# Latent attention with rotary scores: the low rotary products of two score tiles in the two halves of the array's rows, and one set of rotary tables

## The chip, the cores and the metric

The kernel runs on one core of a Trainium2 chip. A core has a matrix engine (PE; its weight loads are listed apart as PEld), a vector engine (DVE), an activation engine (ACT), GpSimd (POOL) and a queue of its own for issuing transfers (SP). Each engine runs its instructions in order and waits on counting semaphores. The metric is the device time of one execution in microseconds; less is better.

## The reference

One transformer block on x of 2048 rows and 512 columns. The layer norm of x is xn. The result is x + attention(xn) + linear(xn), where the linear part uses a weight rounded to three values and adds a bias. The attention has 16 heads, a shared latent key of 128 columns and a shared rotary key of 64 columns:

```python
q = (x @ wq.T).reshape(B, S, N_HEADS, QK_HEAD)
q_nope, q_pe = (q[..., :NOPE], q[..., NOPE:])
q_pe = apply_rope(q_pe, cos, sin)
kv = x @ wkv_a.T
kv_lat, k_pe = (kv[..., :KV_RANK], kv[..., KV_RANK:])
k_pe = apply_rope(k_pe[:, :, None, :], cos, sin)[:, :, 0, :]
q_lat = jnp.einsum('bshd,hdc->bshc', q_nope, wkv_b_h[:, :NOPE])
kv_cache = rmsnorm(kv_lat, kv_norm_w)
scores = (jnp.einsum('bshc,btc->bsht', q_lat, kv_cache) + jnp.einsum('bshr,btr->bsht', q_pe, k_pe)) * SCALE
attn = jax.nn.softmax(jnp.where(causal, scores, NEG_INF), axis=-1)
out_lat = jnp.einsum('bsht,btc->bshc', attn, kv_cache)
out = jnp.einsum('bshc,hdc->bshd', out_lat, wkv_b_h[:, NOPE:])
return out.reshape(B, S, N_HEADS * VDIM) @ wo.T
```

## The kernel before

The program has two parts. The first (`build_prepare`, up to about 195 us) makes the layer norm, the keys and the folded weights of all heads, and stores them in memory. The second (`build_attention`) is the attention, and the change is nearly all in it.

**Precision by parts.** A float32 number is held as a high part and a low part in the fast 32-bit format (fp32r), and a product a*b is made as high*high + high*low + low*high. So the latent part of a score tile takes three products of 128 rows of the array: (q_h, Kn_h), (q_h, Kn_l), (q_l, Kn_h). The rotary part has 64 rows only. `Kp` holds the high rotary key in partitions 0 to 63 and the low one in 64 to 127; `qp_h` holds the high rotary query twice, `qp_l` the low one twice. So (qp_h, Kp) gives high*high + high*low in one product of 128 rows, and (qp_l, Kp) gives low*high, and low*low with it.

**Tiles and order.** The 2048 queries are cut into NCH = 4 chunks of 512, a chunk into QB = 4 blocks of 128. In chunk j, a head has 4(j+1) score tiles ("units" u): query block i = u // (j+1) against key block b = u % (j+1), of 512 keys, or of 128(i+1) keys on the diagonal (b = j), which also gets a product with the mask (L1000). Over 16 heads and 4 chunks that makes 640 tiles. Two PSUM buffers, `p_score[u % 2]`, take the tiles in turn.

`walk` goes from head to head; one call of `step(cur, prev, nxt)` on each engine does the scores of head cur, the transposes and value products of head prev, and the projections of head nxt. On PE a step is, for every unit u: `scores(cur, u)` (L996, L1000), `transposes(prev, u)` of the probabilities (L1013, four of 128 columns, fewer in the last four tiles), `values(prev, u-2)` (L1025, three products); the rotary projection of nxt (L976, 12 products) stands once in every second step, at the unit that `rotary_unit` gives (half way; unit 1 in chunk 0). Behind the units come the latent projection of nxt (four groups of three products, L976, "q" below) with the last two value groups between them, and then the output projection (12 products, L1036).

**DVE** does for every unit, in this order: `copy_scores` (L1081), which waits for `scored`, copies the tile into `probs` and takes its maximum; on the diagonal `neg_max` (L1087); then `split_tile` (L1093), the low part of the transposed tile of prev, for which ACT makes the high part (L1173). The five rotary operations of nxt (L1104, L1108) follow behind the unit of the rotary projection, three in one unit and two in the next. **PE waits** for DVE in two ways here: `scores(u)` waits until tile u-2 is copied, `values(k)` until tile k is split, and `transposes(k)` until tile k-3 is split.

**SP** loads the weights of each head a head ahead; the tables `cosT` and `sinT` of a chunk have two buffers each, and are loaded with the residual `acc` long before the chunk.

Of the kernel before, what the change touches and what calls it, by code (L numbers as in the profile page):

```python
# [120 lines left out]
def build_prepare(nc, t, keep, stored):  # L121
# [4 lines left out]
    with ExitStack() as ctx:  # L126
        def sb(name, shape, dt=F32):
            return ctx.enter_context(nc.sbuf_tensor(name, shape, dt))
# [7 lines left out]
        ident, xT, residual = keep["ident"], keep["xT"], keep["acc0"]  # L136
        Wq, Wp, Wv = keep["Wq"], keep["Wp"], keep["Wv"]
        w_ffn = sb("w_ffn", [P, IT, D])
        ffnT_h = sb("ffnT_h", [P, IT, D], F32R)
# [270 lines left out]
        def _(act):  # L410
# [59 lines left out]
            act.dma_start(rows[:, D:], t["kv_norm_w"].rearrange("(a n) -> a n", a=1)).then_inc(s_const, 16)  # L470
            act.dma_start(keep["order_f32"][:, :], t["order"]).then_inc(s_const, 16)
            act.dma_start(keep["mask_f32"][:, :], t["mask"]).then_inc(s_const, 16)
            act.dma_start(w_ffn[:, :, :], t["w_ffn"].rearrange("(a p) i -> p a i", p=P)).then_inc(s_w, 16)
            act.wait_ge(s_const, 16 * 6)
            act.activation(keep["mask"][:, :], keep["mask_f32"][:, :], ACT.Copy)
            act.activation(keep["ident16"][:, :], ident[:, :], ACT.Copy)
            act.activation(order[:, :], keep["order_f32"][:, :], ACT.Copy).then_inc(s_order, 1)

# [325 lines left out]
def build_attention(nc, t, keep, stored):  # L804
    with ExitStack() as ctx:
# [10 lines left out]

        cosT = [keep["cosT"], sb("cosT1", [P, CW])]
        sinT = [keep["sinT"], sb("sinT1", [P, CW])]
        acc = [keep["acc0"], sb("acc1", [P, QB, D])]
# [26 lines left out]
        p_result = p_tr + [p_out]  # L846

        xT_in = sem("xT_in")
        tables_in = sem("tables_in")
        wq_in = [sem(f"wq_in{i}") for i in range(2)]  # L850
        wp_in = sem("wp_in")
# [28 lines left out]
        def _(sp):  # L880
# [33 lines left out]


            for i in range(2):
# [7 lines left out]
            for j in range(NCH):  # L924
                if j:
                    load_rotary((j, 0, 0))
                    load_q((j, 0, 0))
                    load_v((j - 1, H // 2 - 1, 0))
                    load_chunk(j)
                    load_q((j, 0, 1))  # L930
                    load_v((j - 1, H // 2 - 1, 1))
                load_rotary((j, 1, 0))
                for p in range(2):
                    load_q((j, 1, p))
                    if j:
                        load_v((j, 0, p))
                if j:
                    store_chunk(j - 1)
                if j + 1 < NCH:
                    load_tables(j + 1)  # L940
# [11 lines left out]
        def _(pe):  # L952
# [26 lines left out]

            def scores(pos, u):  # L980
                j, p = pos[0], pos[2]
                i, b = u // (j + 1), u % (j + 1)
                width = P * (i + 1) if b == j else CW
                if u == 0:
# [4 lines left out]
                rows, keys = slice(i * P, (i + 1) * P), slice(b * CW, b * CW + width)  # L989
                out = p_score[u % 2]  # L990
# [48 lines left out]
            def step(cur, prev, nxt):  # L1039
# [29 lines left out]
            for it in range(IT):  # L1069
                project_latent((0, 0, 0), it)  # L1070
            walk(nc, ENG.PE, step)

        @block.vector
        def _(dve):
# [21 lines left out]
            def rotate(pos, op):  # L1096

                if op == 0:
                    if first_of_chunk(pos):
                        need(dve, tables_in, 48 * pos[0])  # L1100
# [3 lines left out]
                    dve.tensor_tensor(rot_cos[:, :], p_rot[:, :], cosT[pos[0] % 2][:, :], ALU.mult)  # L1104
                else:
                    q = op - 1
                    to, of = slice(HALF * q, HALF * (q + 1)), slice(HALF * (q ^ 1), HALF * ((q ^ 1) + 1))
                    last = dve.tensor_tensor(rot_sin[to, :], p_rot[of, :], sinT[pos[0] % 2][of, :], ALU.mult)  # L1108
                    if op == 4:
                        last.then_inc(rot_read, 1)  # L1110
# [10 lines left out]
            def accumulate(pos):  # L1121
                g, p = heads_before(pos), pos[2]
                a = acc[pos[0] % 2]
                dve.wait_ge(exped, rows_before(pos) + QB)
                need(dve, accumulated, QB * g)
# [138 lines left out]
def build(nc, t):  # L1264
    with ExitStack() as ctx:
        def sb(name, shape, dt=F32):
# [5 lines left out]
            "mask": sb("mask_bf16", [P, P], BF16),  # L1272
            "mask_f32": sb("mask_f32", [P, P]),
            "order_f32": sb("order_f32", [P, ROPE]),
            "Kn_h": sb("Kn_h", [P, S], F32R),
# [68 lines left out]
```

## Time and profile before

| | us |
|---|---|
| median of three runs | 1972.43 (1972.4 to 1973.72) |
| span of the profiled execution | 1972.3 |
| PE busy in it | 1911.1 (97%) |
| PE weight loads | 1596.1 (81%) |
| DVE busy | 1277.8 (65%) |
| ACT busy | 887.7 (45%) |
| POOL busy | 317.0 (16%) |
| chain that ended last, PE's share | 81% |

The span of the profiled execution and the median of the runs are the same within 0.2 us, so a change of the span is read as a change of the time. A product of 512 columns is listed with about 0.39 us, but the next one starts 0.23 us behind it: they overlap in the engine. What one costs is the distance from start to start, not its listed duration.

### The profile page before, as it was taken

The page shows a single profiled execution, that of the slowest core. Times are in us where ns is not written, and L with a number is a line of the kernel's source. Part 1 is how long each engine was busy: PE and PEld are TensorE (multiplying, and loading weights), DVE is VectorE, ACT ScalarE, POOL GpSimd, SP SyncE. Part 2 cuts the span into 40 slices and gives each one's busy share as a digit, 9 for nine tenths or more (in the row PEclk, how much of TensorE's full clock was granted, in tenths as well). Part 3 has the DMA queues.
Part 4 walks back from the last instruction along what each step waited for, and adds up shares of the span by engine and source line. Part 5 has one row for each costly group of instructions (what it writes and reads, how often), then busy time and mean ns, then how long its engine had stood idle before and what let it go on. Part 6 is the DMA issues. An engine that isn't in the chain of part 4 may idle for free.

```text
span 1972.3 us, 32409 instructions
## 1 busy us (share of the span) xinstructions
PE 1911.1 (97%) x10414; PEld 1596.1 (81%) x10414; DVE 1277.8 (65%) x3031; ACT 887.7 (45%) x1646; POOL 317.0 (16%) x313
## 2 busy tenths in 40 slices
PE   5999899999999999999999999999999999999998
PEld 4887677778888888888888888878888888888886
DVE  5665566666666666666666676666666566666665
ACT  4444344444444444444444444444444444444443
POOL 4565222221111111111001110010010110101100
PEclk9898999999999999999999999999999999999999
DMA  5896322233111112210101011212000010011000
GB/s 181 314 311 219 109 95 85 96 128 107 63 64 53 53 64 96 97 54 32 53 32 43 32 53 42 76 34 74 22 32 32 31 43 21 32 32 34 19 11 22
DMA packets 53076, 147.46 MB, mean 75 GB/s; under 512 B 4834, under 2 KB 17379, under 8 KB 51492
## 3 DMA queue, kind: packets, MB, share of 16 engines
q1 hardware_dynamic: 52208, 145.71, 21.7%
q10 hardware_dynamic: 820, 1.15, 0.2%
q8 instruction: 26, 0.43, 0.1%
q14 instruction: 22, 0.18, 0.0%
HBM read 112.23 MB, written 34.60 MB: 74 GB/s over the span
## 4 chain that ended last, share of the span: by engine, by line
PE 81%; DVE 4%; issue 3%; POOL 2%; ACT 0%; DVEq 0%; POOLq 0%; ACTq 0%
PE p_score L996 31%; PE p_out L1025 18%; PE p_tr L1013 12%; PE p_lat L976 7%; PE p_tr L1036 6%; PE p_rot L976 4%; DVE rot_sin L1108 2%; PE p_out L1036 2%; DVE probs L1081 1%; PE p_score L1000 1%; POOL qp_l L1247 1%; POOL qp_l L1250 1%; POOL rotated L1236 1%; DVE pT_l L1093 0%; DVE rot_cos L1104 0%
## 5 line engine op out<-in xcount | busy, mean ns | idle before, releaser
L1173 ACT ACTIVATE pT_h<-p_tr 128x512 fp32r<-128x512 f32 (+3 forms) x640 | 339.0, 531 | 790.6 <-PE p_tr L1013 788.5
L1081 DVE TENSOR_SCALAR_CACHE_REDUCE probs<-p_score 128x512 f32<-128x512 f32 (+3 forms) x640 | 388.7, 607 | 168.6 <-PE p_score L996 109.7
L1093 DVE TENSOR_TENSOR pT_l<-p_tr,pT_h 128x512 fp32r<-128x512 f32 (+3 forms) x640 | 390.4, 610 | 159.5 <-ACT pT_h L1173 152.7
L1013 PE MATMUL p_tr<-ident,probs 128*128 128x128 f32 x2176 | 343.0, 273 | 0.0
L1164 ACT ACTIVATE probs<-probs,neg_max 128x128 f32<-128x128 f32 (+15 forms) x256 | 307.5, 1201 | 70.3 <-DVE neg_max L1087 69.0
L1013 PEld LDWEIGHTS p_tr<-ident,probs 128*128 128x128 f32 x2176 | 260.4, 140 | 52.5
L1025 PE MATMUL p_out<-pT_h,V_h 128*128 128x512 f32 (+3 forms) x640 | 274.7, 429 | 6.8 <-DVE pT_l L1093 6.8
L996 PE MATMUL p_score<-Kn_h,q_h 128*128 128x512 f32 (+3 forms) x640 | 241.3, 377 | 3.3 <-DVE q_l L1115 3.3
L996 PE MATMUL p_score<-Kp,qp_h 128*128 128x512 f32 (+3 forms) x640 | 234.5, 366 | 8.6 <-POOL qp_l L1250 8.6
L1025 PE MATMUL p_out<-pT_h,V_l 128*128 128x512 f32 (+3 forms) x640 | 234.9, 367 | 0.0
L1025 PE MATMUL p_out<-pT_l,V_h 128*128 128x512 f32 (+3 forms) x640 | 233.5, 365 | 0.0
L996 PE MATMUL p_score<-Kn_h,q_l 128*128 128x512 f32 (+3 forms) x640 | 233.4, 365 | 0.0
L996 PE MATMUL p_score<-Kp,qp_l 128*128 128x512 f32 (+3 forms) x640 | 233.3, 365 | 0.0
L996 PE MATMUL p_score<-Kn_l,q_h 128*128 128x512 f32 (+3 forms) x640 | 232.1, 363 | 0.0
L1236 POOL TENSOR_TENSOR rotated<-rot_cos,rot_sin 128x512 f32<-128x512 f32 x32 | 41.1, 1284 | 1113.4 <-DVE rot_sin L1108 1113.4
L976 PE MATMUL p_lat<-xT,Wq 128*128 128x512 f32 x768 | 203.2, 397 | 0.0
L976 PEld LDWEIGHTS p_lat<-xT,Wq 128*128 128x128 f32 x768 | 138.2, 188 | 21.9
L996 PEld LDWEIGHTS p_score<-Kp,qp_h 128*128 128x128 f32 x640 | 120.8, 189 | 29.2 <-POOL qp_l L1250 11.0
L996 PEld LDWEIGHTS p_score<-Kn_h,q_h 128*128 128x128 f32 x640 | 120.6, 188 | 27.3 <-DVE q_l L1115 5.4
L1247 POOL TENSOR_TENSOR qp_l<-rotated,qp_h 64x512 fp32r<-64x512 f32 x64 | 82.4, 1287 | 362.3 <-ACT qp_h L1192 362.3
L996 PEld LDWEIGHTS p_score<-Kn_l,q_h 128*128 128x128 f32 x640 | 121.0, 189 | 22.7
L1130 DVE SCALAR_TENSOR_TENSOR acc<-p_tr,inv_sum,acc 128x512 f32<-128x512 f32 x192 | 132.6, 745 | 8.9 <-PE p_tr L1036 3.0
(143 smaller groups left out, 2676.4 us busy)
## 6 DMA issues: line engine op xcount, KB each, us to landing
Wq<-wq_scr SPq DMA_DIRECT2D x62, 512.0 KB, 3.3
Wv<-wv_scr SPq DMA_DIRECT2D x62, 512.0 KB, 3.2
Wp<-wp_scr SPq DMA_DIRECT2D x31, 512.0 KB, 3.3
wq_scr<-Wq SPq DMA_DIRECT2D x16, 512.0 KB, 5.3
wv_scr<-Wv SPq DMA_DIRECT2D x16, 512.0 KB, 5.3
xT_scr<-xT SPq DMA_DIRECT2D x3, 2048.0 KB, 10.1
xT<-xT_scr SPq DMA_DIRECT2D x3, 2048.0 KB, 7.8
x_in<-in_x SPq DMA_DIRECT2D x4, 1024.0 KB, 7.0
```

Source lines behind the costliest of these rows:

```text
L976: mm = pe.matmul(out, weights[:, w, it, :], xT[:, x, it, :], start=(it == 0 and k == 0), stop=(it == IT - 1 and k == 2))
L996: mm = pe.matmul(out[:, 0:width], q[p][:, rows], kk[:, keys], start=(k == 0), stop=(k == 4 and b < j))
L1013: mm = pe.transpose(p_tr[k % PT_RING][:, i * P:(i + 1) * P], probs[p][:, i, k * P:(k + 1) * P], ident[:, :])
L1025: mm = pe.matmul(p_out[:, cols], v[:, k, :], pt[r][:, cols], start=(k == 0 and a == 0), stop=(last and a == 2))
L1036: mm = pe.matmul(out[:, :], o[:, rows], Wv[p][:, w, :], start=(k == 0), stop=(k == 2))
L1081: dve.tensor_scalar(probs[p][:, i, b * CW:b * CW + width], p_score[u % 2][:, 0:width], SCALE, LOWEST, ALU.mult, ALU.max, accum_out=part_ma ...
L1093: dve.tensor_tensor(pT_l[r][:, cols], p_tr[r][:, cols], pT_h[r][:, cols].bitcast(F32), ALU.subtract).then_inc(pT_split, 1)
L1130: dve.scalar_tensor_tensor(out=a[:, i, :], in0=p_result[i][:, :], scalar=inv_sum[p][:, i:i + 1], in1=a[:, i, :], op0=ALU.mult, op1=ALU.add ...
L1164: act.activation(probs[p][:, i, 0:width], probs[p][:, i, 0:width], ACT.Exp, bias=neg_max[p][:, i:i + 1], scale=1.0, accum_out=row_sum[p][: ...
L1173: act.activation(pT_h[r][:, cols], p_tr[r][:, cols], ACT.Copy).then_inc(pT_high, 1)
L1236: pool.tensor_tensor(rotated[:, :], rot_cos[:, :], rot_sin[:, :], ALU.add).then_inc(rot_added, 1)
L1247: pool.tensor_tensor(qp_l[p][0:ROPE, :], rotated[own, :], qp_h[p][own, :].bitcast(F32), ALU.subtract).then_inc(qp_ready, 1)
```

## The change

The high products of a tile stay as they are. The low rotary product of a tile is no longer made with the others: behind the high products of every second tile u, `low_scores` makes those of tiles u-1 and u, tile u-1 in rows 0 to 63 of the array with the high key in `Kp`, tile u in rows 64 to 127 with a copy of the high key that lies in those partitions (`Kp_twin`, loaded once by a transfer at the start of the attention). The low*low term goes away with it. Both tiles' `scored` are raised there. The mask product goes ahead of the low product. The copy needs room: the rotary tables have one buffer instead of two, and are loaded behind the chunk's `xT` and ahead of the second weight load, the residual is loaded apart (`load_residual`), and two float32 constants live in the first part only.

```diff
-        cosT = [keep["cosT"], sb("cosT1", [P, CW])]
-        sinT = [keep["sinT"], sb("sinT1", [P, CW])]
+        cosT, sinT = keep["cosT"], keep["sinT"]
...
+        Kp_twin = sb("Kp_twin", [P, S], F32R)
...
             def load_tables(j):
 
-
-                need(sp, rot_read, H // 2 * (j - 1))
+                sp.wait_ge(rot_read, H // 2 * j)
+                sp.dma_start(cosT[:, :], t["cosT"][j]).then_inc(tables_in, 16)
+                sp.dma_start(sinT[:, :], t["sinT"][j]).then_inc(tables_in, 16)
+
+            def load_residual(j):
+
                 need(sp, result_out, 16 * (j - 1))
-                sp.dma_start(cosT[j % 2][:, :], t["cosT"][j]).then_inc(tables_in, 16)
-                sp.dma_start(sinT[j % 2][:, :], t["sinT"][j]).then_inc(tables_in, 16)
-                sp.dma_start(acc[j % 2][:, :, :], t["acc_scr"][j]).then_inc(tables_in, 16)
+                sp.dma_start(acc[j % 2][:, :, :], t["acc_scr"][j]).then_inc(acc_in, 16)
...
+            sp.dma_start(Kp_twin[ROPE:P, :].bitcast(F32), Kp[0:ROPE, :].bitcast(F32)).then_inc(twin_in, 16)
...
                     load_chunk(j)
+                    load_tables(j)
                     load_q((j, 0, 1))
...
-                for k, (q, kk) in enumerate(((q_h, Kn_h), (q_h, Kn_l), (q_l, Kn_h), (qp_h, Kp), (qp_l, Kp))):
+                for k, (q, kk) in enumerate(((q_h, Kn_h), (q_h, Kn_l), (q_l, Kn_h), (qp_h, Kp))):
                     if u == 0 and k == 3:
 
                         pe.wait_ge(qp_ready, 2 * heads_before(pos) + 2)
-                    mm = pe.matmul(out[:, 0:width], q[p][:, rows], kk[:, keys], start=(k == 0),
-                                   stop=(k == 4 and b < j))
-                if b == j:
-
-                    mm = pe.matmul(out[:, width - P:width], ident16[:, :], mask[:, :], start=False, stop=True)
-                mm.then_inc(scored, 1)
+                    pe.matmul(p_score[u % 2][:, 0:width], q[p][:, rows], kk[:, keys], start=(k == 0), stop=False)
+                if last:
+
+                    pe.matmul(p_score[u % 2][:, width - P:width], ident16[:, :], mask[:, :], start=False, stop=False)
+
+            def low_scores(pos, u):
+                p = pos[2]
+                for v, half, kk in ((u, slice(0, ROPE), Kp), (u + 1, slice(ROPE, P), Kp_twin)):
+                    rows, keys, width, _ = place(pos, v)
+                    pe.matmul(p_score[v % 2][:, 0:width], qp_l[p][half, rows], kk[half, keys], start=False,
+                              stop=True).then_inc(scored, 1)
...
                     if cur:
                         scores(cur, u)
+                        if u % 2:
+                            low_scores(cur, u - 1)
                     if u < tiles:
                         transposes(prev, u)
...
+            pe.wait_ge(twin_in, 16)
             walk(nc, ENG.PE, step)
...
                 if first_of_chunk(pos):
+                    need(dve, acc_in, 16 * pos[0])
```

What stands on PE at the first pair of tiles of a head in the loop of chunk 3, before (the names are tile and operands; ISA and REGISTER_ALU rows are waits and counters):

```order
L996 MATMUL p_score<-Kp,qp_h 128x512
L996 MATMUL p_score<-Kp,qp_l 128x512
L1006 ISA
L59 ISA
L1013 MATMUL p_tr<-ident,probs 128x128 x4
L59 REGISTER_ALU
L996 MATMUL p_score<-Kn_h,q_h 128x512
L996 MATMUL p_score<-Kn_l,q_h 128x512
L996 MATMUL p_score<-Kn_h,q_l 128x512
L996 MATMUL p_score<-Kp,qp_h 128x512
L996 MATMUL p_score<-Kp,qp_l 128x512
```

And the same place after:

```order
L1005 MATMUL p_score<-Kp,qp_h 128x512
L1020 ISA
L59 ISA
L1027 MATMUL p_tr<-ident,probs 128x128 x4
L59 REGISTER_ALU
L1005 MATMUL p_score<-Kn_h,q_h 128x512
L1005 MATMUL p_score<-Kn_l,q_h 128x512
L1005 MATMUL p_score<-Kn_h,q_l 128x512
L1005 MATMUL p_score<-Kp,qp_h 128x512
L1014 MATMUL p_score<-Kp,qp_l 128x512
L1014 MATMUL p_score<-Kp_twin,qp_l 128x512
```

The low product of the first tile has moved behind the transposes and the four high products of the second tile; one product of 128 rows each has become one of 64 rows.

PE at the last tile of a head in the same loop, before:

```order
L996 MATMUL p_score<-Kn_h,q_h 128x512
L996 MATMUL p_score<-Kn_l,q_h 128x512
L996 MATMUL p_score<-Kn_h,q_l 128x512
L996 MATMUL p_score<-Kp,qp_h 128x512
L996 MATMUL p_score<-Kp,qp_l 128x512
L1000 MATMUL p_score<-mask_bf,ident 128x128
L1013 MATMUL p_tr<-ident,probs 128x128
```

and after:

```order
L1005 MATMUL p_score<-Kn_h,q_h 128x512
L1005 MATMUL p_score<-Kn_l,q_h 128x512
L1005 MATMUL p_score<-Kn_h,q_l 128x512
L1005 MATMUL p_score<-Kp,qp_h 128x512
L1008 MATMUL p_score<-mask_bf,ident 128x128
L1014 MATMUL p_score<-Kp,qp_l 128x512
L1014 MATMUL p_score<-Kp_twin,qp_l 128x512
L1027 MATMUL p_tr<-ident,probs 128x128
```

Here the scores of the last two tiles become complete together. DVE keeps its order of copies, splits and rotary operations.

## Rows read from the trace of the kernel before

**Rows 1.** The page, part 1: busy us, share of the span, instructions.

```profile
PE 1911.1 (97%) x10414; PEld 1596.1 (81%) x10414; DVE 1277.8 (65%) x3031; ACT 887.7 (45%) x1646; POOL 317.0 (16%) x313
```

**Rows 2.** Who PE waited for: us in total, times, longest.

```profile
PE p_score L996 <- POOL qp_l L1250: 8.6, 11, 4.0
```

**Rows 3.** The page, part 5: the group that the change rewrites.

```profile
L996 PE MATMUL p_score<-Kp,qp_l 128*128 128x512 f32 (+3 forms) x640 | 233.3, 365 | 0.0
```

**Rows 4.** Timeline of PE, chunk 3: start, duration, instruction.

```profile
1498.24 0.40 PE L996 MATMUL p_score<-Kp,qp_h 128*128 128x512 f32 x1
1498.47 0.39 PE L996 MATMUL p_score<-Kp,qp_l 128*128 128x512 f32 x1
1498.70 0.60 PE L1013 MATMUL p_tr<-ident,probs 128*128 128x128 f32 x4
1499.06 0.48 PE L996 MATMUL p_score<-Kn_h,q_h 128*128 128x512 f32 x1
...
1501.71 0.27 PE L996 MATMUL p_score<-Kp,qp_h 128*128 128x128 f32 x1
1501.82 0.27 PE L996 MATMUL p_score<-Kp,qp_l 128*128 128x128 f32 x1
```

**Rows 5.** Timeline of PE around the 64-row products of the first part.

```profile
60.61 0.39 PE L691 MATMUL pF<-ffnT_h,xT 128*128 128x512 f32 x1
60.93 0.63 PE L738 MATMUL pW<-order,wqp_h 64*128 64x64 f32 x4
...
61.94 0.50 PE L691 MATMUL pF<-ffnT_h,xT 128*128 128x512 f32 x1
62.27 0.39 PE L691 MATMUL pF<-ffnT_l,xT 128*128 128x512 f32 x1
```

**Rows 6.** The same stretch, weight loads (PEld).

```profile
60.39 0.19 PEld L691 LDWEIGHTS pF<-ffnT_h,xT 128*128 128x128 f32 x1
60.93 0.52 PEld L738 LDWEIGHTS pW<-order,wqp_h 64*128 64x128 f32 x4 [0.35 <-issue]
61.37 0.52 PEld L738 LDWEIGHTS pW<-order,wqp_l 64*128 64x128 f32 x4
61.94 0.19 PEld L691 LDWEIGHTS pF<-ffnT_h,xT 128*128 128x128 f32 x1
```

**Rows 7.** Weight loads at the same place one round later.

```profile
98.68 0.52 PEld L738 LDWEIGHTS pW<-order,wqp_h 64*128 64x128 f32 x4 [0.35 <-issue]
...
99.68 0.19 PEld L691 LDWEIGHTS pF<-ffnT_h,xT 128*128 128x128 f32 x1
```

**Rows 8.** Timeline of DVE at the start of a head, chunk 3.

```profile
1497.95 0.68 DVE L1081 TENSOR_SCALAR_CACHE_REDUCE probs<-p_score 128x512 f32<-128x512 f32 x1
1498.56 0.08 DVE L1081 DVE_READ_ACCUMULATOR probs<-p_score 128x1 f32 x1
```

**Rows 9.** Timeline of PE at the end of a head, chunk 3.

```profile
1530.76 0.40 PE L996 MATMUL p_score<-Kp,qp_h 128*128 128x512 f32 x1
...
1531.22 0.23 PE L1000 MATMUL p_score<-mask_bf,ident 128*128 128x128 bf16 x1
...
1533.00 0.22 PE L1025 MATMUL p_out<-pT_h,V_h 128*128 128x128 f32 x1
```

**Rows 10.** Timeline of DVE at the end of the same head.

```profile
1531.49 0.69 DVE L1081 TENSOR_SCALAR_CACHE_REDUCE probs<-p_score 128x512 f32<-128x512 f32 x1 [1.08 <-PE p_score L1000]
...
1532.32 0.29 DVE L1093 TENSOR_TENSOR pT_l<-p_tr,pT_h 128x128 fp32r<-128x128 f32 x1
```

**Rows 11.** Timeline of DVE, the rotary operations of chunk 1's first head.

```profile
426.11 0.69 DVE L1104 TENSOR_TENSOR rot_cos<-p_rot,cosT 128x512 f32<-128x512 f32 x1 [2.37 <-issue]
426.81 2.79 DVE L1108 TENSOR_TENSOR rot_sin<-p_rot,sinT 32x512 f32<-32x512 f32 x4
```

**Rows 12.** Timeline of SP at the end of chunk 0.

```profile
414.54 0.33 SPq L900 DMA_DIRECT2D xT<-xT_scr  x1
```

**Rows 13.** The page, part 6: issues, KB each, median us from issue to landing.

```profile
xT<-xT_scr SPq DMA_DIRECT2D x3, 2048.0 KB, 7.8
```

More of the change, by code:

```diff
@@ L137, in build_prepare @@
         Wq, Wp, Wv = keep["Wq"], keep["Wp"], keep["Wv"]
+        mask_f32 = sb("mask_f32", [P, P])
+        order_f32 = sb("order_f32", [P, ROPE])
         w_ffn = sb("w_ffn", [P, IT, D])
@@ L470, in _ @@
             act.dma_start(rows[:, D:], t["kv_norm_w"].rearrange("(a n) -> a n", a=1)).then_inc(s_const, 16)
-            act.dma_start(keep["order_f32"][:, :], t["order"]).then_inc(s_const, 16)
-            act.dma_start(keep["mask_f32"][:, :], t["mask"]).then_inc(s_const, 16)
+            act.dma_start(order_f32[:, :], t["order"]).then_inc(s_const, 16)
+            act.dma_start(mask_f32[:, :], t["mask"]).then_inc(s_const, 16)
             act.dma_start(w_ffn[:, :, :], t["w_ffn"].rearrange("(a p) i -> p a i", p=P)).then_inc(s_w, 16)
             act.wait_ge(s_const, 16 * 6)
-            act.activation(keep["mask"][:, :], keep["mask_f32"][:, :], ACT.Copy)
+            act.activation(keep["mask"][:, :], mask_f32[:, :], ACT.Copy)
             act.activation(keep["ident16"][:, :], ident[:, :], ACT.Copy)
-            act.activation(order[:, :], keep["order_f32"][:, :], ACT.Copy).then_inc(s_order, 1)
+            act.activation(order[:, :], order_f32[:, :], ACT.Copy).then_inc(s_order, 1)
             act.wait_ge(s_aT, 1)
@@ L846, in build_attention @@
         p_result = p_tr + [p_out]
+        twin_in = sem("twin_in")
         xT_in = sem("xT_in")
         tables_in = sem("tables_in")
+        acc_in = sem("acc_in")
         wq_in = [sem(f"wq_in{i}") for i in range(2)]
@@ L939, in _ @@
                 if j + 1 < NCH:
-                    load_tables(j + 1)
+                    load_residual(j + 1)
                 with nc.Fori(2, H // 2, engines=[ENG.SP]) as m:
@@ L978, in product, with place, scores @@
                 return mm
-            def scores(pos, u):
-                j, p = pos[0], pos[2]
+            def place(pos, u):
+                j = pos[0]
                 i, b = u // (j + 1), u % (j + 1)
                 width = P * (i + 1) if b == j else CW
+                return slice(i * P, (i + 1) * P), slice(b * CW, b * CW + width), width, b == j
+            def scores(pos, u):
+                p = pos[2]
+                rows, keys, width, last = place(pos, u)
                 if u == 0:
@@ L988, in scores @@
                 need(pe, copied, tiles_before(pos) + u - 1)
-                rows, keys = slice(i * P, (i + 1) * P), slice(b * CW, b * CW + width)
-                out = p_score[u % 2]
-                for k, (q, kk) in enumerate(((q_h, Kn_h), (q_h, Kn_l), (q_l, Kn_h), (qp_h, Kp), (qp_l, Kp))):
+                for k, (q, kk) in enumerate(((q_h, Kn_h), (q_h, Kn_l), (q_l, Kn_h), (qp_h, Kp))):
                     if u == 0 and k == 3:
                         pe.wait_ge(qp_ready, 2 * heads_before(pos) + 2)
-                    mm = pe.matmul(out[:, 0:width], q[p][:, rows], kk[:, keys], start=(k == 0),
-                                   stop=(k == 4 and b < j))
-                if b == j:
-                    mm = pe.matmul(out[:, width - P:width], ident16[:, :], mask[:, :], start=False, stop=True)
-                mm.then_inc(scored, 1)
+                    pe.matmul(p_score[u % 2][:, 0:width], q[p][:, rows], kk[:, keys], start=(k == 0), stop=False)
+                if last:
+                    pe.matmul(p_score[u % 2][:, width - P:width], ident16[:, :], mask[:, :], start=False, stop=False)
+            def low_scores(pos, u):
+                p = pos[2]
+                for v, half, kk in ((u, slice(0, ROPE), Kp), (u + 1, slice(ROPE, P), Kp_twin)):
+                    rows, keys, width, _ = place(pos, v)
+                    pe.matmul(p_score[v % 2][:, 0:width], qp_l[p][half, rows], kk[half, keys], start=False,
+                              stop=True).then_inc(scored, 1)
             def transposes(pos, k):
@@ L1099, in rotate @@
                     if first_of_chunk(pos):
-                        need(dve, tables_in, 48 * pos[0])
+                        need(dve, tables_in, 32 * pos[0])
                     dve.wait_ge(rot_projected, pairs_before(pos) + 1)
                     need(dve, rot_added, pairs_before(pos))
-                    dve.tensor_tensor(rot_cos[:, :], p_rot[:, :], cosT[pos[0] % 2][:, :], ALU.mult)
+                    dve.tensor_tensor(rot_cos[:, :], p_rot[:, :], cosT[:, :], ALU.mult)
                 else:
@@ L1107, in rotate @@
                     to, of = slice(HALF * q, HALF * (q + 1)), slice(HALF * (q ^ 1), HALF * ((q ^ 1) + 1))
-                    last = dve.tensor_tensor(rot_sin[to, :], p_rot[of, :], sinT[pos[0] % 2][of, :], ALU.mult)
+                    last = dve.tensor_tensor(rot_sin[to, :], p_rot[of, :], sinT[of, :], ALU.mult)
                     if op == 4:
@@ L1123, in accumulate @@
                 a = acc[pos[0] % 2]
+                if first_of_chunk(pos):
+                    need(dve, acc_in, 16 * pos[0])
                 dve.wait_ge(exped, rows_before(pos) + QB)
@@ L1272, in build @@
             "mask": sb("mask_bf16", [P, P], BF16),
-            "mask_f32": sb("mask_f32", [P, P]),
-            "order_f32": sb("order_f32", [P, ROPE]),
             "Kn_h": sb("Kn_h", [P, S], F32R),
```

## The prediction

> **What bounds the kernel now.** I read the busy shares first, then who PE waited for, then the timelines of PE. PE is busy 1911.1 of 1972.3 us [rows 1], and its longest named wait is 8.6 us in total, 4.0 of them once, before the first head's rotary product [rows 2]. So from the attention's start PE runs one product behind the other, and an edit is worth what it takes from or adds to PE's own row of starts. DVE, at 65%, has slack as a mean, but its work has due times within a head; that matters below.
>
> What PE pays for a product is the distance of starts. Two products of 512 columns start 0.23 us apart (1498.24 to 1498.47), two of 128 columns 0.11 us (1501.71 to 1501.82) [rows 4]. Four weight loads of the 64-row kind span 0.52 us where one takes 0.19, so loads follow each other by 0.11 us, as much as that 0.11, with 64 rows as with 128 [rows 6]. A narrow product is thus bound by its load. For 256 and 384 columns I take 0.12 and 0.175, between these two.
>
> **What the change removes.** 640 products (qp_l, Kp) [rows 3] in 320 pairs. Per head the pairs are, by columns of first and second tile: chunk 0 (128,256), (384,512); chunk 1 (512,128), (512,256), (512,384), (512,512); chunk 2 (512,512), (128,512), (512,256), (512,512), (384,512), (512,512); chunk 3 four (512,512) and the four of chunk 1. If the two halves ran wholly beside each other and nothing else changed, a pair would cost the wider product only, and the narrower would be saved: 0.285, 0.635, 1.10 and 1.56 us per head in the four chunks, 3.58 us x 16 heads = 57 us. That is the whole of the possible gain.
>
> **What it adds on PE: two changes between 128 rows and 64 rows per pair.** The trace of before has such changes, in the first part, around the 64-row products of L738. Within one kind, a product's weights are loaded beside the product ahead of it: the load at 60.39 [rows 6] serves the product at 60.61 [rows 5]. At the change this stops. The 512-column product starts at 60.61 [rows 5], and the first 64-row load only at 60.93 [rows 6]: 0.32 us behind, that is 0.21 us of streaming (0.23 at most) and some 0.10 us in which the array runs empty. The load itself then lies open: 0.11 us. So the first half product streams 0.43 us behind its predecessor, where 0.23 would do: 0.20 us for going in. Going out: the last 64-row load starts at 61.37 + 3 x 0.11 = 61.70 and its product 0.03 later, the next full load at 61.94, 0.21 behind the product, and that product streams another 0.11 later, at 62.05; its follower at 62.27 [rows 5], a normal 0.22 later, confirms it. Unswitched it would have been 61.84: 0.21 us for going out. The same distances, with the same idle of 0.35, come back one round later (98.68, 99.68) [rows 7], so it is no accident of a wait. The Trainium skill states the cause: by its page TensorEngine Tiling, section "Key Properties", changing the tiling mode drains the TensorE. The trace agrees with it, at 0.20 us each way.
>
> Now a pair of (512,512), counted from the start of the last full product ahead of it. Load of the first half at 0.32, its product streams from 0.43; load of the second 0.11 later, its product streams from 0.54 beside the first. The next full load (the transposes') comes 0.32 behind that, at 0.86, and the transposes stream from 0.97. Before it was 3 x 0.23 = 0.69. That is +0.28 us for a pair although the two products do overlap. With the narrow tile second, the first tile's end decides: 0.43 + 0.32 + 0.11 = 0.86 against 0.57 to 0.635, and between that and the second's end +0.28 to +0.29. With the narrow tile first, (128,512), the saved product was only 0.11: 0.97 against 0.57, +0.40; (384,512) +0.33, (128,256) +0.40. Per head 0.73 + 1.13 + 1.85 + 2.25 = 5.96 us, x 16 = **95 us**. Bounds: if the second half's load ran beside the first's, up to 0.11 per pair less, all pairs together 68 us. If the two halves did not overlap at all, about 0.40 per pair, 128 us. I take 95, since loads of one kind follow each other at 0.11 [rows 6]. The removed low*low term costs or saves nothing of its own: it was part of the same product.
>
> **What it adds through DVE: both tiles of a pair become complete together.** DVE holds copy, split, copy, split in this order, and now idles through the first tile and then has all four in a row. Copy 0.61 + 0.08 [rows 8], say 0.70 to 0.73 with what follows it; split 0.60 to 0.62 (the copies and splits of 512 columns have like durations). The copy starts about 0.04 us behind the end of the last product, 0.43 behind its start: the mask product of 0.23 at 1531.22 [rows 9] is followed by the copy at 1531.49 [rows 10]. Let a be the moment at which the first half product streams. Three places become tight:
>
> First, the third tile of a head. It needs tile 0 copied. Before, the copy began at 1497.95 [rows 8] and was done by 1498.64, with PE due at 1499.06 [rows 4]. Between the pair and tile 2 there is only one set of transposes and no value product yet. PE: second half a + 0.11, transposes' first load a + 0.43, three more and tile 2's at a + 0.87, streaming a + 0.98. DVE: copy from a + 0.43 to a + 1.13; PE sees it 0.05 later and loads 0.11: a + 1.29. A wait of 0.31 us; in chunk 1 with its narrow tile 1, 0.44. 32 x 0.31 + 16 x 0.44 = 17 us; in chunk 0 the copy has 128 columns, about 1 us in all.
>
> Second, the end of a head. The last value group (128 columns) was at 1533.00, 1.78 behind the mask product [rows 9]; its split began at 1532.32 and took 0.29 [rows 10], so it had 0.39 us to spare. With s the start of the last high rotary product: mask s + 0.23 and 0.05 of streaming, first half load s + 0.38, a = s + 0.49, transposes' load s + 0.92, streaming s + 1.03, last value group 1.71 later (1.78 less the mask's 0.07): s + 2.74. DVE: copy s + 0.92, split of 256 columns s + 1.65 to 2.00, last copy s + 2.00, and from there to the end of the split 1.12 (1531.49 to 1532.61): s + 3.12, with PE's load s + 3.28. A wait of 0.55 us, in the 45 heads of chunks 1 to 3 whose predecessor is in the same chunk: 25 us. In chunk 0 another projection group lies between, and no wait comes.
>
> Third, the step with the rotary operations, 23 times in chunks 1 to 3. The four sine operations take 2.79 us, 0.70 each [rows 11], and three rotary ones stand between the copies of a pair's tiles. Copy and split to a + 1.78, three rotary to a + 3.88, second copy to a + 4.61, PE's start a + 4.77. PE reaches the tile that needs it after transposes, values, a tile, transposes and values, 3.2 us behind the transposes at a + 0.54: a + 3.75. A wait of about 1.0 us: 22 us. Chunk 1, where the next pair ends the head, adds 0.4 x 7 = 3 us, chunk 0 about 0.75 x 8 = 6 us. All places together **74 us**. None of this is on the path before; it is the cover that the change removes.
>
> **What costs nothing.** The twin's transfer (512 KB) has from the attention's start to the first scores, and behind them the 4.0 us wait for POOL [rows 2]. The rotary tables (two of 256 KB) now follow xT, issued at 414.54 [rows 12] with 7.8 us to landing for four times their size [rows 13], thus by about 422.4, and the tables some 2 us later; the first rotary operation was at 426.11 [rows 11]. If this cover went, it would cost some 2 us three times. POOL and ACT keep their work and follow PE.
>
> **Sum.** 1972.3 + 95 + 74 = 2141 us; span and median are the same within 0.2. I forecast 2140.
>
> **Rivals.** (a) The waits for DVE do not add up, because DVE catches up in other time than I count; the switches alone remain: 1972.4 + 95 = 2067. For it: DVE is 65% busy. Against: the order on DVE is fixed and PE is not ahead of it at these places.
>
> (b) The second half's weights load beside the first's. The pairs cost 68 us; DVE is then asked 0.1 us earlier at some 115 places, +11: 1972.4 + 68 + 85 = 2125. Rows 6 show 0.11 between loads of the same half only, so it is open. The Trainium skill speaks for it: TensorE: Matmul & The Clock Gate, Part 3, section "The mechanism", has loads of different row groups overlap and products start about 4 ns apart; no row here shows it.
>
> (c) The change doesn't do what it says: the halves run one after the other. The pairs cost 128 us, and the waits shrink by 0.1 to 0.2 at each place to some 50: 1972.4 + 128 + 50 = 2150.
>
> (d) Faster: the switch costs nothing, since the half loads go beside the running product as full loads do, and each pair gives back up to 57/320 = 0.18 us. It decides in favour if switches and DVE's waits together stay under that 0.18 per pair: 1972.4 - 57 = 1915. Rows 5 to 7 speak against it. Even with free switches DVE's waits would be met sooner (about 100 us at the three places), which gives 2015, slower.
>
> **How the numbers follow.** Forecast 0.52 (its own range 2105 to 2175), (a) 0.17, (b) 0.13, (c) 0.10, (d) 0.03 at 1915 and 0.04 at 2015, no difference 0.01. From 2050 to 2185 the forecast, (b), (c) and most of (a) lie inside. Faster by over 0.2% 0.03, within 0.2% (what a measurement of this kernel can tell) 0.01, slower 0.96.
>
> **What would show it.** In the profile after: half loads 0.32 us behind the last full product's start, and transposes' loads 0.32 behind the second half's; second half's start 0.11 behind the first's (0.00 for b, 0.2 for c); PE waits for the copies (tile 2 of a head, and the tile behind the rotary operations) and for the last split, of 0.3, 1.0 and 0.55 us. Full loads beside half products would make the whole wrong. No such waits with the switches there would leave (a).

## The result and the profile after

| | us |
|---|---|
| before, median (4 runs) | 1973.08 |
| changed, median (4 runs, 2109.34 to 2112.61) | 2110.77 |
| ratio, with 95% interval | 1.0698 (1.0684 to 1.0712) |
| span of the profiled execution after | 2111.0 |

The change makes the kernel 7% slower, by 138 us. The forecast was 2140. The mean granted clock of PE is 0.989 in both profiled executions, so the clock has no part in it. The page of after, part 1, with the columns of [rows 1]:

```profile
PE 1998.1 (95%) x10414; PEld 1549.9 (73%) x10414; DVE 1240.7 (59%) x3031; ACT 885.9 (42%) x1646; POOL 316.6 (15%) x313
```

PE has as many instructions as before and is listed as busy for 87 us more; the other engines have the same instructions, with more idle time. DVE is listed with 37 us less, since its instructions now stand in bursts and overlap more; their durations add up to 1399 us before and 1394 us after. Who PE waited for:

```profile
PE p_score L1005 <- DVE probs L1098: 28.6, 72, 0.9
PE p_out L1039 <- DVE pT_l L1110: 27.2, 54, 2.4
PE p_score L1005 <- POOL qp_l L1269: 8.6, 11, 4.0
```

The first row is new, the third is as in [rows 2]. The second had this before:

```profile
PE p_out L1025 <- DVE pT_l L1093: 6.8, 18, 0.9
```

These idle times start at the listed end of the product ahead. A product is listed with 0.40 us where the next one would start after 0.23, so a wait costs about 0.17 us more than is listed here.

**The pair.** PE and its weight loads at the first pair of a head in chunk 3 of after, the place that answers to the first four of [rows 4] (start, duration, instruction):

```profile
1604.53 0.40 PE L1005 MATMUL p_score<-Kp,qp_h 128*128 128x512 f32 x1
1604.85 0.49 PE L1014 MATMUL p_score<-Kp,qp_l 64*128 64x512 f32 x1
1604.86 0.49 PE L1014 MATMUL p_score<-Kp_twin,qp_l 64*128 64x512 f32 x1
1605.28 0.66 PE L1027 MATMUL p_tr<-ident,probs 128*128 128x128 f32 x4
1606.13 0.50 PE L1005 MATMUL p_score<-Kn_h,q_h 128*128 128x512 f32 x1 [0.20 <-DVE probs L1098]
```

```profile
1604.30 0.19 PEld L1005 LDWEIGHTS p_score<-Kp,qp_h 128*128 128x128 f32 x1
1604.85 0.18 PEld L1014 LDWEIGHTS p_score<-Kp,qp_l 64*128 64x128 f32 x1 [0.37 <-issue]
1604.85 0.18 PEld L1014 LDWEIGHTS p_score<-Kp_twin,qp_l 64*128 64x128 f32 x1
1605.28 0.42 PEld L1027 LDWEIGHTS p_tr<-ident,probs 128*128 128x128 f32 x4 [0.24 <-issue]
```

The first half load starts 0.32 us behind the full product, as in [rows 5 and 6]. But both halves' loads start together, and so do both products. The transposes' load comes 0.42 us behind the second half, by my reading 0.11 for the half's open load and 0.32 for streaming and emptying, as on the way in. The load of a transpose is short: where a full load leaves 0.11 us open, this one leaves 0.06, since the group of four lasts 0.66 us here and 0.60 before [rows 4]. So the transposes stream from 1605.34, 0.81 us behind the last full product, where three products of 0.23 made 0.69: **+0.12 us for a pair of (512,512)**. Read in the same way (medians of each kind of pair, before against after): with a tile of 384 columns +0.16 to +0.18, with one of 128 or 256 +0.21 to +0.24. Per head and chunk that is 0.40, 0.74, 0.99 and 1.21 us, x 16 = **53 us**.

**The waits for DVE.** DVE at the same place of after:

```profile
1603.81 0.74 DVE L1149 SCALAR_TENSOR_TENSOR acc<-p_out,inv_sum,acc 128x512 f32<-128x512 f32 x1
1605.38 0.69 DVE L1098 TENSOR_SCALAR_CACHE_REDUCE probs<-p_score 128x512 f32<-128x512 f32 x1 [0.83 <-PE p_score L1014]
1606.00 0.08 DVE L1098 DVE_READ_ACCUMULATOR probs<-p_score 128x1 f32 x1
1606.00 0.69 DVE L1110 TENSOR_TENSOR pT_l<-p_tr,pT_h 128x512 fp32r<-128x512 f32 x1
```

Before, the copy of tile 0 followed the accumulation without a gap [rows 8]. Now DVE stands idle for 0.83 us, copies until 1606.08, and PE starts tile 2 at 1606.13. Its listed 0.20 us is a wait of 0.45, by the distance from the last transpose. Second place, the end of a head, which answers to [rows 9]:

```profile
1639.88 0.39 PE L1005 MATMUL p_score<-Kp,qp_h 128*128 128x512 f32 x1
1640.11 0.23 PE L1008 MATMUL p_score<-mask_bf,ident 128*128 128x128 bf16 x1
...
1642.33 0.28 PE L1039 MATMUL p_out<-pT_h,V_l 128*128 128x256 f32 x1
1642.93 0.33 PE L1039 MATMUL p_out<-pT_h,V_h 128*128 128x128 f32 x1 [0.32 <-DVE pT_l L1110]
```

The last value group came 1.78 us behind the mask product before; now it comes 2.82 behind it. Of this, 0.60 is the last step, where 0.11 between narrow products would do; most of the rest is the pair, which now stands behind the mask product. Third place, the rotary operations, PE and DVE of the same head:

```profile
1628.73 0.40 PE L1039 MATMUL p_out<-pT_h,V_l 128*128 128x512 f32 x1
1629.88 0.45 PE L1005 MATMUL p_score<-Kn_h,q_h 128*128 128x384 f32 x1 [0.75 <-DVE probs L1098]
```

```profile
1625.82 0.69 DVE L1098 TENSOR_SCALAR_CACHE_REDUCE probs<-p_score 128x512 f32<-128x512 f32 x1 [4.95 <-PE p_score L1014]
...
1626.44 0.69 DVE L1110 TENSOR_TENSOR pT_l<-p_tr,pT_h 128x512 fp32r<-128x512 f32 x1
1627.04 0.68 DVE L1121 TENSOR_TENSOR rot_cos<-p_rot,cosT_sb 128x512 f32<-128x512 f32 x1
1627.73 1.38 DVE L1125 TENSOR_TENSOR rot_sin<-p_rot,sinT_sb 32x512 f32<-32x512 f32 x2
1629.12 0.69 DVE L1098 TENSOR_SCALAR_CACHE_REDUCE probs<-p_score 128x512 f32<-128x512 f32 x1
```

DVE idles for 4.95 us and then has the whole row to do, three rotary operations between the copies. The product at 1629.88 should have started 0.23 behind 1628.73; it is 0.92 late, and its open load adds 0.1. The heads of before and after laid beside each other, instruction by instruction, give:

- Third tile: 0.45 us in each of 48 heads, 22 us.
- End of the head: 0.53 to 0.59 us in 35 of the 45 heads. In seven heads of chunk 1 with rotary operations PE already waited 0.46 us here before (part of the 6.8 above), and only 0.2 is new. In the last heads of chunks 1 and 2, where the rotary operations stand close to the end, the wait grew by 1.9 and 1.0. Together 24 us.
- Rotary place: 1.0 to 1.2 us in 21 heads, seven in each of chunks 1 to 3, 24 us.
- Everything else, above all chunk 0 (6 us), the value groups behind the rotary place and the first heads of the chunks: some 13 us.

That is 83 us of waits. With the pairs' 53 us it makes 136 of 138 us.

### The profile page after: what moved, and what is told of

Read it like the earlier page. It is cut to its first block, busy times and chain, and to the rows that moved or that the text cites. A ratio compares the mean times of both kernels' runs of the same rounds, so it can differ in the third digit from the quotient of the medians.

```text
span 2111.0 us, 32409 instructions
## 1 busy us (share of the span) xinstructions
PE 1998.1 (95%) x10414; PEld 1549.9 (73%) x10414; DVE 1240.7 (59%) x3031; ACT 885.9 (42%) x1646; POOL 316.6 (15%) x313
## 4 chain that ended last, share of the span: by engine, by line
PE 74%; DVE 8%; issue 5%; POOL 2%; ACT 0%; DVEq 0%; POOLq 0%; ACTq 0%
PE p_score L1005 24%; PE p_out L1039 15%; PE p_tr L1027 11%; PE p_score L1014 6%; PE p_lat L983 6%; PE p_tr L1050 5%; PE p_rot L983 4%; DVE rot_sin L1125 3%; DVE probs L1098 3%; DVE pT_l L1110 2%; PE p_out L1050 2%; PE p_score L1008 1%; DVE rot_cos L1121 1%; POOL qp_l L1266 1%; POOL qp_l L1269 1%
## 5 line engine op out<-in xcount | busy, mean ns | idle before, releaser
L1027 PE MATMUL p_tr<-ident,probs 128*128 128x128 f32 x2176 | 359.8, 281 | 0.0
L1027 PEld LDWEIGHTS p_tr<-ident,probs 128*128 128x128 f32 x2176 | 250.9, 141 | 109.8 <-issue 72.5
L1039 PE MATMUL p_out<-pT_h,V_h 128*128 128x512 f32 (+3 forms) x640 | 279.6, 437 | 28.1 <-DVE pT_l L1110 27.2
L1005 PE MATMUL p_score<-Kn_h,q_h 128*128 128x512 f32 (+3 forms) x640 | 247.1, 386 | 32.2 <-DVE probs L1098 28.6
L1039 PEld LDWEIGHTS p_out<-pT_h,V_h 128*128 128x128 f32 x640 | 124.7, 195 | 49.2 <-DVE pT_l L1110 43.1
L1014 PE MATMUL p_score<-Kp,qp_l 64*128 64x512 f32 (+1 forms) x320 | 152.2, 476 | 0.0
L1014 PE MATMUL p_score<-Kp_twin,qp_l 64*128 64x512 f32 (+3 forms) x320 | 145.0, 453 | 0.0
```

Source lines behind the costliest of these rows:

```text
L1005: pe.matmul(p_score[u % 2][:, 0:width], q[p][:, rows], kk[:, keys], start=(k == 0), stop=False)
L1014: pe.matmul(p_score[v % 2][:, 0:width], qp_l[p][half, rows], kk[half, keys], start=False, stop=True).then_inc(scored, 1)
L1027: mm = pe.transpose(p_tr[k % PT_RING][:, i * P:(i + 1) * P], probs[p][:, i, k * P:(k + 1) * P], ident[:, :])
L1039: mm = pe.matmul(p_out[:, cols], v[:, k, :], pt[r][:, cols], start=(k == 0 and a == 0), stop=(last and a == 2))
```

## The experiments

**The price of a switch by itself.** From the kernel before: the low product of each tile in 64 rows, where it stood.

```diff
                 for k, (q, kk) in enumerate(((q_h, Kn_h), (q_h, Kn_l), (q_l, Kn_h), (qp_h, Kp), (qp_l, Kp))):
...
-                    mm = pe.matmul(out[:, 0:width], q[p][:, rows], kk[:, keys], start=(k == 0),
+                    part = slice(0, ROPE) if k == 4 else slice(0, P)
+                    mm = pe.matmul(out[:, 0:width], q[p][part, rows], kk[part, keys], start=(k == 0),
```

> The kernel before, with each tile's low rotary product made in rows 0 to 63 alone (64 rows instead of 128), at its old place right behind the high ones; low times low is left out, as in the change. Nothing is paired and no tile becomes complete later. Theory (each change between 128 and 64 rows costs PE a drain and an open weight load): in the trace of the change the half product starts 0.33 us behind the full one and the transposes stream some 0.37 us behind the half product's streaming, so a 512-column tile costs 0.34 us more, a diagonal one 0.30 to 0.34; 640 tiles give about +215 us, near 2188 us, without new waits for DVE. Rival (the half products are cheap, and only the lateness of the scores costs): within 5 us of before, 1973.

Measured: 2173.08 us against 1971.55, ratio 1.1021 (1.1003 to 1.104), +201.5 us although each low product now has half the rows. PE and PEld of this kernel:

```profile
1501.19 0.40 PE L997 MATMUL p_score<-Kp,qp_h 128*128 128x512 f32 x1
1501.52 0.49 PE L997 MATMUL p_score<-Kp,qp_l 64*128 64x512 f32 x1
1501.94 0.66 PE L1014 MATMUL p_tr<-ident,probs 128*128 128x128 f32 x4
```

```profile
1501.52 0.18 PEld L997 LDWEIGHTS p_score<-Kp,qp_l 64*128 64x128 f32 x1 [0.37 <-issue]
1501.94 0.42 PEld L1014 LDWEIGHTS p_tr<-ident,probs 128*128 128x128 f32 x4 [0.24 <-issue]
```

The same two idle stretches of the loads, 0.37 and 0.24, with one half product between them. So the switch is paid for the change of rows, not for the pairing. For a tile of 512 columns it is 0.35 us as expected; the diagonal tiles came to 0.24 to 0.30 instead of 0.30 to 0.34, which is most of the 14 us that my figure was too high.

**What the overlap is worth.** The change with both low products in the same half:

```diff
-                for v, half, kk in ((u, slice(0, ROPE), Kp), (u + 1, slice(ROPE, P), Kp_twin)):
+                for v, half, kk in ((u, slice(0, ROPE), Kp), (u + 1, slice(0, ROPE), Kp)):
```

> The change, but both low products of a pair use rows 0 to 63, so that they can't run beside each other; the number of switches and the order stay. Theory (the halves do overlap in the change, and it is worth the narrower product): the pairs cost 57 us more (0.23 for two of 512 columns), and DVE's waits shrink by up to 0.23 us at some 116 places, 27 us: near 2140 us, and the second product starts about 0.2 us behind the first instead of 0.003. Rival (the halves don't overlap in truth, the trace's starts mislead): the same as the change, 2110.

Measured: 2141.28, ratio 1.086 (1.0842 to 1.0878), 30 us more than the change. The two products and the transposes behind them:

```profile
1599.72 0.40 PE L1005 MATMUL p_score<-Kp,qp_h 128*128 128x512 f32 x1
1600.05 0.73 PE L1014 MATMUL p_score<-Kp,qp_l 64*128 64x512 f32 x2
1600.71 0.66 PE L1027 MATMUL p_tr<-ident,probs 128*128 128x128 f32 x4
```

From the full product to the transposes 0.99 us, 0.75 in the change. The halves do run beside each other there, and it is worth one product of 0.23; the instructions laid beside those of the change give 55 us more for the pairs and 28 us less of waits, a net of 27 (30 between the medians).

**The order without the switch.** The change with both low products in 128 rows, behind each other, as late as in the change:

```diff
-                for v, half, kk in ((u, slice(0, ROPE), Kp), (u + 1, slice(ROPE, P), Kp_twin)):
+                for v, half, kk in ((u, slice(0, P), Kp), (u + 1, slice(0, P), Kp)):
```

> The change with its order, but the two low products of a pair use all 128 rows (with low times low) and lie behind each other: no change of rows, only the lateness of both tiles' scores. Theory (DVE's waits are there by themselves): after the change PE waits some 0.45 us at the third tile of a head, 0.56 us at its end, 1.2 us behind the rotary operations; here the transposes come 0.08 us later behind the pair, so 0.37 x 48 + 0.48 x 45 + 1.1 x 23 + 6 for chunk 0 = 71 us, near 2044 us. Rival (the waits come from the switches, the order alone costs nothing): 1973. Rival (all of the loss is the order): 2110.

Measured: 2062.7, ratio 1.0462 (1.0444 to 1.0479), +91 us. There is no switch. The row of PE starts is as dense as before but for the waits and one thing more; first the waits:

```profile
1501.09 0.62 PE L1014 MATMUL p_score<-Kp,qp_l 128*128 128x512 f32 x2
1501.55 0.60 PE L1027 MATMUL p_tr<-ident,probs 128*128 128x128 f32 x4
...
1504.50 0.40 PE L1039 MATMUL p_out<-pT_h,V_l 128*128 128x512 f32 x1
1505.57 0.44 PE L1005 MATMUL p_score<-Kn_h,q_h 128*128 128x384 f32 x1 [0.67 <-DVE probs L1098]
```

The other thing is the mask product, which the change puts ahead of the low products. Here is a last pair of this run, and below it the same place before:

```profile
1047.84 0.39 PE L1005 MATMUL p_score<-Kp,qp_h 128*128 128x512 f32 x1
1048.07 0.23 PE L1008 MATMUL p_score<-mask_bf,ident 128*128 128x128 bf16 x1
1048.11 0.71 PE L1014 MATMUL p_score<-Kp,qp_l 128*128 128x512 f32 x2
1048.65 0.27 PE L1027 MATMUL p_tr<-ident,probs 128*128 128x128 f32 x1
```

```profile
1003.25 0.23 PE L1000 MATMUL p_score<-mask_bf,ident 128*128 128x128 bf16 x1
1003.32 0.28 PE L1013 MATMUL p_tr<-ident,probs 128*128 128x128 f32 x1
```

Between a full product and the transposes the mask product takes 0.07 us. Here it and two low products take 0.58 us, where two products alone take 0.46: 0.12 for the mask, 0.05 more than before. In the pairs with halves it costs nothing more: with a mask +0.11, without one +0.12 for (512,512). Over all heads this is 8 us of the 91. The waits of the profiled execution come to 77 us, 21 at the third tile, 21 at the end of the head, 22 at the rotary place, the rest as in the change. (This execution was 5 us faster than the median of its kernel.) So the lateness of the scores alone is the larger half of the loss. It was 19 us more than I expected, and the mask accounts for 8 of them.

**What costs nothing.** The change with the low products of before, so that only the transfer of the twin, the single tables and the residual's own load remain (the whole of `scores` and `step` on PE as before).

> The change without its products: the twin's transfer, the single rotary tables behind xT, the residual loaded apart, and the low products as before (128 rows, at their old place). Theory: all of it lies beside other work, within 1 us of before, 1973. Rival (the tables come late at a chunk's start, or the twin at the start): +2 us for each of three chunks, up to 1980.

Measured: 1972.42 (10 runs) against 1971.55, ratio 1.0002 (0.9992 to 1.0011). No difference.

**The rotary place.** In chunks 2 and 3, DVE's rotary operations behind second tiles only:

```diff
+def rotary_slot(nxt, units, op):
+    r = rotary_unit(nxt, units)
+    if units >= 12 and r % 2 == 0:
+        return r + 1 + 2 * (op // 3)
+    return min(r + op // 3, units - 1)
...
-                        if nxt and nxt[2] == 0 and u == min(rotary_unit(nxt, units) + op // 3, units - 1):
+                        if nxt and nxt[2] == 0 and u == rotary_slot(nxt, units, op):
```

> The change, but in chunks 2 and 3 DVE does three rotary operations behind the second tile of the pair and two behind the second tile of the next pair, where before three stood between the two tiles' copies and two behind them. Theory (PE waits there because the second copy stands behind three rotary operations): the wait of some 1.2 us goes in the 15 heads of chunks 2 and 3 that have it (the first heads of chunk 3 excepted), 15 x 1.2 = 18 us: near 2093 us; chunk 1 as in the change. Rival (DVE is short of time in all, and the wait moves to the next pair): within 3 us of 2110.

Measured: 2097.41, ratio 1.0634 (1.0616 to 1.0652), 13 us less than the change; the wait for `probs` fell to this:

```profile
PE p_score L1012 <- DVE probs L1105: 17.3, 58, 0.9
```

The cause is right. It gave less than I had put in, 1.2 us in each of 15 heads: it is 14 heads, and laid beside the change each of the seven in chunk 3 gives 1.3 us, each of the seven in chunk 2 only 0.8, because 0.4 us comes back there ahead of the last two value groups.

**The waits taken away by the order.** From the change: both tiles' products in one piece, then both tiles' transposes and values (the run's second version has both low products in 128 rows, as in the order without the switch); the rotary operations behind second tiles, and in chunk 1 the rotary projection two units earlier.

```diff
-                    if cur:
+                    if cur and u % 2 == 0:
                         scores(cur, u)
-                        if u % 2:
-                            low_scores(cur, u - 1)
+                        scores(cur, u + 1)
+                        low_scores(cur, u)
```

> The change with a pair's high and low products in one piece and then both tiles' transposes and value groups (instead of one set between the two tiles), and the rotary operations behind second tiles, the rotary projection of chunk 1 two units earlier. Between the pair and the next tile PE now has about twice the work. Theory (what is left without DVE's waits is the pairs' own price, 53 us summed from the rows of after): 1973 + 53 + some 7 for the third tile of a head = 2033 us. Rival (the rest of the loss is not in DVE's waits): 2090 or more.

> The same order as the run before it (both tiles' scores in one piece), but the low products use all 128 rows, behind each other, no switch. Theory (this order leaves hardly a wait, and there is no switch): 1973 to 1980 us, and its distance to the run with the halves is the price of the switches net of the overlap, about 53 us. Rival (the order itself costs): 2000 or more, and the distance is smaller than 40.

Measured: 2075.68, ratio 1.0522 (1.0505 to 1.054) with the halves, and 2034.52, ratio 1.0325 (1.0308 to 1.0342), with 128 rows. Both expectations failed, by 43 and by 54 us. For the first the time lies between the theory and its rival; for the second the rival said 2000 or more, which came true. The trace of the second shows why:

```profile
1550.26 0.39 PE L1012 MATMUL p_score<-Kp,qp_h 128*128 128x512 f32 x1
1551.40 0.33 PE L1012 MATMUL p_score<-Kn_h,q_h 128*128 128x128 f32 x1 [0.75 <-DVE probs L1105]
```

```profile
1549.28 0.08 DVE L1105 DVE_READ_ACCUMULATOR probs<-p_score 128x1 f32 x1
1550.05 0.69 DVE L1117 TENSOR_TENSOR pT_l<-p_tr,pT_h 128x512 fp32r<-128x512 f32 x1 [0.68 <-ACT pT_h L1199]
1550.65 0.68 DVE L1105 TENSOR_SCALAR_CACHE_REDUCE probs<-p_score 128x512 f32<-128x512 f32 x1
```

The first pair of a head has no value products behind it yet. The fourth tile needs tile 1 copied, and that copy stands behind a split which itself waited 0.68 us for ACT. Over all heads the waits at the fourth tile come to 41 us in either run. I had looked at the third tile and not at the fourth.

**With these waits gone too.** The same order from the third tile on; the first two tiles of each head singly, with 128 rows, as before the change (but with the mask product still ahead of the low one):

```diff
-                    if cur and u % 2 == 0:
+                    if cur and u < 2:
+                        scores(cur, u)
+                        low_alone(cur, u)
+                    if cur and u >= 2 and u % 2 == 0:
```

> As the run with both tiles' scores in one piece and halves, but the first two tiles of each head are made singly and wholly as before the change (low product with 128 rows, right behind the high ones); pairs in halves from the third tile on. That run still waited some 0.7 to 0.9 us at the fourth tile of each head, where the copy of tile 1 stood behind that of tile 0 and the accumulation of the head before. Theory (with these waits gone only the pairs' own price is left): the first pairs take 0.23, 0.235, 0.12 and 0.12 us a head out of the 53 us, 11 us, so 1972 + 42 = 2014 us, plus at most 10 for what remains at the rotary operations of chunk 0. Rival (the order with two tiles in one piece costs by itself): 2030 or more.

> The same with the low products of the pairs in 128 rows behind each other: the order alone, without a switch. Theory: no waits are left, 1972 to 1982 us, and the distance to the run with halves is the net price of 256 pairs, 42 us. Rival: 1990 or more.

Measured: 2017.38, ratio 1.0231 (1.0214 to 1.0248) with the halves; 1987.02, ratio 1.0074 (1.0057 to 1.0091) with 128 rows. What PE waits for at scores and values with the halves, and what the weight loads (PEld) wait for:

```profile
PE p_score L1012 <- POOL qp_l L1284: 8.6, 11, 4.0
...
PE p_out L1051 <- DVE pT_l L1125: 2.3, 9, 0.6
```

```profile
PEld p_score L1012 <- DVE probs L1113: 5.8, 29, 0.3
```

and the loads of the version with 128 rows:

```profile
PEld p_out L1051 <- DVE pT_l L1125: 10.6, 17, 0.8
...
PEld p_score L1012 <- DVE probs L1113: 7.4, 38, 0.3
```

On PE itself no wait for `probs` is left, and at the loads a few short ones. With the halves the 45.5 us above before agree with the price of 256 pairs, 42 by the rows of after. But the version with 128 rows is 15 us above before, not 0 to 10, some 10 of them in chunk 2, and the distance between the two is 30 us, as it was 41 in the pair of runs before where 53 were expected: 12 us too little both times.

The instructions of before and of these two runs laid beside each other account for this. Without any wait, the row of starts of the version with 128 rows is 12 us longer than before, 6 of them in chunk 2. The mask product ahead of a full product makes a part of it everywhere; the largest single place is the pair of chunk 2 whose first tile has 128 columns, 0.22 us in each head. The version with halves is 47 us longer (and has 2 us less of waits), so the halves themselves cost 35, not 42: I had counted their price against the order of before and not against this order. The other 5 us are waits: the longest are for the last split in seven heads of chunk 2, 0.6 us each with 128 rows and 0.4 with the halves, whose switches seem to fill a part of that time. No run of this study is faster than the kernel before.

## Why the prediction was right, and where it was off

**The bound and the sign: right.** PE is the bound, and what a pair adds to its row of starts is added to the time.

**The switch: right in kind, too large in size.** 95 us were forecast for the pairs, the rows of after give 53. The way in was right, 0.32 us behind the full product's start. Two terms were mis-sized. The second half's load was put 0.11 us behind the first's, from loads of one half [rows 6]; it goes beside it (1604.85 both). That was rival (b), 68 us, and in this point it holds, with 2 to 5 ns between the two products' starts over all 320 pairs. The Trainium skill, TensorE: Matmul & The Clock Gate, Part 3, section "The mechanism", has loads of different row groups overlap and gives about 4 ns from one product's start to the next; the trace agrees. And the open load on the way out was taken from a full product's load, 0.11; behind the pair stand transposes, whose load leaves 0.06 open, 0.05 x 320 = 16 us less. The general case fits the runs: 201.5 us for 640 pairs of switches around single products.

**The whole gain of 57 us for free overlap: right as a bound.** The same-half run shows 0.23 us for a pair of 512 columns.

**DVE's waits: right, a little too small.** 74 us forecast, some 83 found. Third tile 0.31 (0.44 in chunk 1) forecast, 0.45 everywhere; end of the head 0.55, found 0.53 to 0.59 in 35 heads; rotary place 1.0, found 1.0 to 1.2. In chunks 2 and 3 the third tile's wait was too small by about the 0.11 and 0.05 us by which the pair was too long, which fits that PE was there earlier than I counted; in chunk 1 and at the end of the head no such difference shows, so this reading is argued and not shown. That none of these waits was on the path before is not quite right: PE already waited 0.46 us for the last split in seven heads of chunk 1. The sum for the end of the head still came out, 24 us for 25, because two last heads of chunks wait longer. With the overlapping loads (b) gave 85 for the waits, and its 68 for the pairs was still 15 too much.

**The total: luck in part.** The two terms were off in opposite directions, 42 us too much for the pairs and 9 too little for the waits. With the pairs sized as measured and the waits as forecast the sum would have been 2100 us, below the forecast's own range.

**What costs nothing: right**, shown by the run with only the transfers, 1.0002.

**The rivals.** (a), the waits do not add up, falls: the order without a switch costs 91 us by itself. (c), the halves don't overlap, falls. (d), the switch is free, falls by the run with single half products; its second part, that with DVE's waits even a free switch loses, is borne out by the order without a switch, whose 91 us are more than the 57 that free switches could give back. The likeliest case and (b) were the same but for the loads, and (b) was the nearer: the time is 14 us under its 2125 and 29 under 2140.

**Whether the parts add up.** 53 us of pairs and 91 us for the order alone make 144, not 138. Some 8 of the 91 are the mask product ahead of a full product, which pairs with halves don't pay; without them it is 136. In the traces the change has 83 us of waits and the order alone 77.

## What to carry to other kernels

Half-array products pay for the way in and the way out, here about 0.35 us together, so one pair of them between full products loses even though the two overlap. By these numbers two such pairs in a row would win a little (an estimate: 0.35 + 2 x 0.23 = 0.81 us against 4 x 0.23 = 0.92), but that takes accumulators that are free, and no run here tried it. A product that completes a tile should not be moved behind the next tile's: the engine that copies then gets its work in bursts, and the mean share of busy time (65% here) says little of the due times in a burst. To find the price before a change, look for the same switch elsewhere in the trace, and ask whose weights are loaded behind it. And price an edit against the order it leaves, not against the old one: moving the mask product cost 8 us in the run without a switch.

## What the runs showed of the hardware

Not expected: weight loads for the two halves start within a few nanoseconds of each other and take together as long as one (1604.85 and 1604.85, the products listed 0.49 us long where a full one has 0.40), while loads of one half follow each other by 0.11 us [rows 6]. And the open load behind a switch depends on what is loaded: 0.11 us for a weight of a 32-bit product [rows 5 and 6], 0.06 us for that of a transpose (the second transpose starts at 1605.44, 0.17 behind the first at 1605.28, where 0.11 is usual). A small bf16 product costs by its neighbours: 0.07 us between a full product and transposes, 0.12 between two full products (1048.07 to 1048.65 with two products of 0.23 in it).
